# Output turned back by pairs of channels in the two depthwise convolutions of a ConvNeXt-like block

## The chip, the cores and the metric

One core of one Trainium2 chip runs the kernel. The metric is the time of one execution on the device in microseconds.

## What is computed

x has 16 images of 96 channels of 56 x 56 pixels, fp32. Two layers follow each other:

```python
y = depthwise_conv_7x7(x, dw_w) + dw_b               # padding 3
y = layernorm_over_channels(y) * ln_w + ln_b
y = gelu(y @ w1 + b1)                                # 96 -> 384
y = gamma * (y * nx) + beta + y                      # nx: norm over pixels by its mean over channels
y = x + (y @ w2 + b2)                                # 384 -> 96
xq = clip(floor(y * 2**16) / 2**16)
out = depthwise_conv_3x3(xq, power_of_two(w)) + bq   # padding 1
```

## The kernel before

The program has three stages, and each goes through DRAM: the first convolution with running mean and variance over the channels (results in `y_scratch` and `stats_scratch`), the two matrix products by images (`z_scratch`), and the second convolution (`out`). The change touches the convolutions alone. PE is TensorE, DVE is VectorE, ACT is ScalarE, POOL is GpSimd and SP is SyncE, which issues most transfers.

Both convolutions are written by functions of the same names with a stage `S` (`"a"` the first, `"c"` the second). A depthwise convolution goes channel by channel over all images. A **batch** is four channels, there are 24 batches, and `p`, the batch number's lowest bit, picks one of two buffers. For each channel:

- SP loads its rows into `xin` (L369). PE turns the input (`tin`, L636) for two channels at a time: 16 transposes, each of a half of the array, the two halves one beside the other, into PSUM banks 0 and 1. ACT copies and rounds the turned input to `xt_h` (L788, two halves of the images), and DVE takes the low part `xt_l` = turned input minus `xt_h` (L995, two halves).
- `convolve` (L641) does the passes (L664): matrix products of 112 x 128 tables with 464 columns of turned input, over the full array. The first convolution has 12 passes a channel, the second 4. PSUM banks 2 and 3 take the channels in turn.
- ACT copies the result to `yt` with the bias (`yt_copy`, L800). In the second convolution the fourth channel of a batch is copied by DVE (L1195).
- `back` (L676, transposes at L682) turns the output: 8 transposes of half an array. It is called two channels later (`two_before`, L303). Its result lies in PSUM banks 4 and 5, in the second convolution by turns in 4, 5 and 6, 7.
- The turned output is copied to `ost`: in the first convolution by ACT (L807), in the second by DVE (L1187), 112 partitions x 448. From there it is stored (L364), in the second convolution the odd channels by a queue of ACT.
- In the first convolution DVE updates mean and deviation for each channel (L1019, L1021, L1023) and POOL sums the squares (L557); ACT rounds the tables (L815) and POOL takes their low part (L542). In the second POOL casts the tables of a batch (L599).

The order of work is written out by hand for each engine in a `body` over the four channels `s` of a batch, and engines meet at semaphores. `TURN` says that the inputs of the next batch's first two channels are turned at `s` = 0, those of the other two at `s` = 2. On PE the waits for what comes after a channel's passes, `back_waits` and `tin_waits`, stand ahead of its last pass:

```python
for n, (k, w, v) in enumerate(todo):
    if n == len(todo) - 1:
        for q in backs:
            back_waits(*q)
        for q in then_turn:
            tin_waits(*q)
```

`tin_waits` waits for the loaded input and, since the banks of the turned input are the same each time, for DVE's low part (L995) of the inputs turned before (semaphore `xt`).

Of the kernel before, what the change touches and what calls it, by code (L numbers as in the profile page):

```python
# [26 lines left out]
ACT = mybir.ActivationFunctionType  # L27
# [67 lines left out]
def build(nc, x, dw_w, dw_b, ln_w, ln_b, w1, b1, grn_gamma, grn_beta, w2, b2, cw, cb, out):  # L95
# [8 lines left out]
    with ExitStack() as ctx:  # L104
# [195 lines left out]
            low, high = slice(0, LSTEP), slice(LSTEP, TW)  # L300
            return ((to[:, 1:RP], odd[:, 0:RP - 1], slice(0, TW)), (to[low, 0], even[low, 0], low), (to[high, 0], odd[high, RP - 1], high))

        def two_before(b, s, p):  # L303

            return (b, s - 2, p) if s >= 2 else (b - 1, s + 2, 1 - p)

        def rows_group(p, s):

            return ost[:, p, s, :].rearrange("p (n r w) -> p n r w", r=2, w=W)

        def evicted(eng, S, b, s):
# [48 lines left out]

        def store_channel(eng, S, dst, b, k, p):

            eng.wait_ge(S["out"], CB * b + k + 1)
            eng.dma_start(image_runs(dst, CB * b + k), ost[:, p, k, :]).then_inc(S[f"st{p}"], 16)  # L364

        def load_runs(eng, src, c, images, p, k, done):
# [20 lines left out]
        def _(sp):  # L387
# [35 lines left out]
            def conv_transfers(S, src, dst, tables):  # L423

                def store(b, k, p):
                    if S is stages["a"] or k % 2 == 0:
                        store_channel(sp, S, dst, b, k, p)

                def body(it, first, last):
                    for p in range(2):  # L430
                        b = 2 * it + p
                        for k in range(CB):
                            if not last:
                                need(sp, S["tin"], 2 * b + k // 2 + 1)
                                load_channel(S, src, b + 2, k, p)
                                if k == 0:
                                    tables(b + 2, p)
                            if k >= 2 and not (first and p == 0):
                                store(b - 1, k - 2, 1 - p)
                            if k < 2 and not first:  # L440
                                store(b - 2, k + 2, p)
                body(0, True, False)
                with sp.Fori(1, NBODY - 2) as it:
                    body(it, False, False)
                body(NBODY - 2, False, False)
                body(NBODY - 1, False, True)
                for n in range(C - 6, C):
                    b, k = divmod(n, CB)
                    store(b, k, b % 2)

# [153 lines left out]
        def _(pe):  # L604
# [13 lines left out]
            def conv_stage(S, kt, slot0, parts, between=None):  # L618
# [49 lines left out]

                outs = p_back["a" if S is stages["a"] else "c"]

                def back_waits(b, s, p):

                    evicted(pe, S, b, s)
                    need(pe, S["out"], CB * b + s + 1 - len(outs))

                def back(b, s, p):  # L676

                    for h in range(RP):
                        for r in range(2):
                            q = LSTEP * r  # L680
                            row = (h + r) % RP if S is stages["a"] else h + r
                            mm = nc.tensor.transpose(outs[s % len(outs)][0:NM, r, W * h:W * h + W],  # L682
                                                     yt[q:q + W, p, s, row], ident[q:q + W, q:q + W])
                    mm.then_inc(S["back"], 1)

                for u in range(2):
# [3 lines left out]
                def body(it, first, last):  # L690
                    for p in range(2):
                        b = 2 * it + p
                        if between and first and p == 1:
                            between()
                        for s in range(G):
                            turns = TURN0 if first and p == 0 else TURN
                            if not (last and p == 1):
                                for u in turns[s]:
                                    tin(b + 1, u, 1 - p)
                            then_turn = [(b + 1, u, 1 - p) for u in turns[s + 1]] if s + 1 < G else [(b + 2, u, p) for u in TURN[0]]  # L700
                            if last and (p == 1 or s + 1 == G):
                                then_turn = []
                            backs = [] if first and p == 0 and s < 2 else [two_before(b, s, p)]
                            convolve(b, s, p, backs, then_turn)
                            for q in backs:
                                back(*q)
                bodies(pe, body)
                for s in (2, 3):
                    back_waits(NBATCH - 1, s, 1)
                    back(NBATCH - 1, s, 1)  # L710


            conv_stage(stages["a"], KA, 0, ((toep_h, xt_h), (toep_h, xt_l), (toep_l, xt_h)), bias_products)


            pe.wait_ge(stages["a"]["out"], C)
            pe.wait_ge(stat_in, 1)
            for g in range(G):
                for r in range(2):
# [44 lines left out]
        def _(act):  # L764
# [14 lines left out]
            def conv_stage(S, bias, scale, rows_too):  # L779
# [10 lines left out]
                def yt_copy(b, s, p):  # L790
                    n = CB * b + s
                    act.wait_ge(S["conv"], n + 1)
                    if isinstance(b, int) and b == 0 and s == 0 and rows_too:
                        act.wait_ge(bias_in, 16)
                    need(act, S["back"], n + 1 - 2 * CB)
# [7 lines left out]
                def out_copy(b, s, p):  # L803
                    act.wait_ge(S["back"], G * b + s + 1)
                    if s == 0:
                        need(act, S[f"st{p}"], 32 * (b - p))
                    nc.scalar.activation(rows_group(p, s), forwards(p_back["a"][0][0:NM], RP), ACT.Identity).then_inc(S["out"], 1)  # L807

                def table_high(b, s, p):
                    if isinstance(b, int) and b == 0:  # L810
# [14 lines left out]
                def body(it, first, last):  # L825
                    for p in range(2):
                        b = 2 * it + p
                        for s in range(G):
                            if not (last and p == 1):
                                for u in (TURN0 if first and p == 0 else TURN)[s]:  # L830
                                    xt_copy(b + 1, u, 1 - p)
                                if rows_too:
                                    for q in (AHEAD0 if first and p == 0 else AHEAD)[s]:
                                        table_high(b + 1, q, 1 - p)
                            if rows_too or s < CB - 1:
                                yt_copy(b, s, p)
                            if rows_too and not (first and p == 0 and s < 2):
                                out_copy(*two_before(b, s, p))
                            if not rows_too and s % 2 and not (first and p == 0):
                                store_channel(act, S, out_v, b - 1, s, 1 - p)  # L840
                bodies(act, body)
                if rows_too:
                    for s in (2, 3):
                        out_copy(NBATCH - 1, s, 1)
# [65 lines left out]
        def _(dve):  # L910
# [269 lines left out]

            S = stages["c"]

            def out_copy(b, s, p):
                dve.wait_ge(S["back"], G * b + s + 1)
                if s == 0:
                    need(dve, S[f"st{p}"], 32 * (b - p))
                dve.tensor_copy(rows_group(p, s), forwards(p_back["c"][s % 2][0:NM], RP)).then_inc(S["out"], 1)  # L1187

            def yt_copy(b, p):
                s = CB - 1  # L1190
                n = CB * b + s
                dve.wait_ge(S["conv"], n + 1)
                need(dve, S["back"], n + 1 - 2 * CB)
                for to, cols, part in turned_back(S, s, p):
                    ins = dve.tensor_scalar(to, cols, -1.0 / FIX, bias_c[part, bass.ds(n, 1)], ALU.mult, ALU.add)  # L1195
                ins.then_inc(S["ytd"], 1)

            def last_batch(b, s, p):
                if s == CB - 1:
                    yt_copy(b, p)  # L1200
                if not (isinstance(b, int) and b == 0 and s < 2):
                    out_copy(*two_before(b, s, p))
            conv_stage(S, last_batch)
            for s in (2, 3):
                out_copy(NBATCH - 1, s, 1)


_INS = ["x", "L0_conv_dw_w", "L0_conv_dw_b", "L0_conv_ln_w", "L0_conv_ln_b", "L0_conv_w1", "L0_conv_b1",
# [19 lines left out]
```

## Time and profile before

| | |
|---|---|
| median of 3 runs | 1029.27 us (1028.33 to 1031.36) |
| profiled execution, its own time | 1031.37 us |
| span in its profile | 1029.5 us |
| PE busy, share of the span | 966.0 us, 94% |
| DVE | 812.9 us, 79% |
| ACT | 764.0 us, 74% |
| POOL | 415.1 us, 40% |
| chain of work that ended last | PE 87%, DMA 4%, DVE 4%, ACT 2% |
| read and written in DRAM | 129.77 MB, 58.25 MB |

Busy shares are means over three stages with different limits, so each stage is to be read by itself. "PEld" is the loading of weights, which runs beside the matrix products. The granted clock is told as a share of 2.4 GHz (1.00) with 1.2 GHz as 0.50. "Idle before" an instruction names what released it. The chain is followed back from the last instruction, at each step to what released it.

### The profile page before, as it was taken

How to read it: one execution, taken by the hardware profiler on the slowest of the kernel's cores; microseconds unless marked ns; L12 is line 12 of the kernel's file. 1: busy time of each engine (PE TensorE's matmuls, PEld its weight loads, DVE VectorE, ACT ScalarE, POOL GpSimd, SP SyncE). 2: the span in 40 equal slices, each digit the busy share in tenths (PEclk: the TensorE clock that was granted, in tenths of full speed). 3: DMA queues.
4: the chain of work that ended last, by engine and by line, in shares of the span. 5: the costliest groups of instructions: out<-in, count | busy, mean ns of one | idle time of the engine just before them, and what ended most of it. 6: DMA issues, size and time to landing. Idle time of an engine off the chain costs nothing.

```text
span 1029.5 us, 22791 instructions
## 1 busy us (share of the span) xinstructions
PE 966.0 (94%) x6342; PEld 693.0 (67%) x6342; DVE 812.9 (79%) x1477; ACT 764.0 (74%) x1379; POOL 415.1 (40%) x357
## 2 busy tenths in 40 slices
PE   5899999999999378999999999999999985999998
PEld 4688888888888266666666666666666633777775
DVE  5678888888888577888888888888888685777876
ACT  3688888888887366799888888899888832666664
POOL 2567777777777145333323333333323110111110
PEclk9899999999999776999999999999999997999999
DMA  7566666666663392555555555555553244899995
GB/s 188 148 206 204 198 192 194 199 194 199 198 199 124 104 248 70 175 165 170 167 169 173 165 162 160 162 173 170 165 172 109 81 141 147 278 294 293 296 297 177
DMA packets 110260, 188.47 MB, mean 183 GB/s; under 512 B 17357, under 2 KB 104036, under 8 KB 107268
## 3 DMA queue, kind: packets, MB, share of 16 engines
q1 hardware_dynamic: 99988, 173.55, 57.2%
q10 hardware_dynamic: 10240, 14.53, 4.7%
q8 instruction: 15, 0.25, 0.1%
q14 instruction: 17, 0.14, 0.1%
HBM read 129.77 MB, written 58.25 MB: 183 GB/s over the span
## 4 chain that ended last, share of the span: by engine, by line
PE 87%; DMA 4%; DVE 4%; ACT 2%; issue 1%; SPq 1%; POOL 1%; ACTq 0%; DVEq 0%; POOLq 0%
PE psum L664 35%; PE psum L740 23%; PE psum L682 7%; PE psum L730 6%; PE psum L731 6%; PE psum L732 6%; PE psum L636 4%; DMA arena<-lines_a 1%; DMA arena_r<-y_scratch 1%; ACT arena L858 1%; DMA arena_r<-stats_scratch 1%; DMA z_scratch<-arena 1%; DVE arena L1082 0%; POOL arena_r L568 0%; DMA lines_a<-arena 0%
## 5 line engine op out<-in xcount | busy, mean ns | idle before, releaser
L664 PE MATMUL psum<-arena_r 112*128 112x464 f32 x1536 | 382.5, 391 | 10.0 <-DVE arena_r L995 6.0
L664 PEld LDWEIGHTS psum<-arena_r 112*128 112x128 f32 x1536 | 277.6, 191 | 56.6 <-issue 9.5
L740 PE MATMUL psum<-arena,w2s 128*96 128x448 f32 x672 | 268.1, 544 | 2.8 <-DVE w2s L1107 2.8
L891 ACT ACTIVATE arena<-psum,b1g 128x448 f32<-128x448 f32 x336 | 202.1, 630 | 61.0 <-PE psum L732 61.0
L568 POOL TENSOR_TENSOR arena_r<-arena,arena_r 96x448 fp32r<-96x448 f32 x112 | 136.6, 1220 | 266.2 <-DVE arena_r L1068 234.6
L740 PEld LDWEIGHTS psum<-arena,w2s 128*96 128x96 f32 x672 | 110.3, 164 | 120.4 <-issue 113.2
L730 PE MATMUL psum<-arena_r,w1h 96*128 96x448 f32 x336 | 153.5, 457 | 15.6 <-POOL arena_r L568 15.6
L800 ACT ACTIVATE arena<-psum,bias_a 64x112 f32<-64x112 f32 (+1 forms) x288 | 107.6, 407 | 64.0 <-PE psum L664 51.1
L557 POOL TENSOR_TENSOR arena<-arena 128x448 f32<-128x448 f32 x96 | 110.5, 1151 | 98.3 <-DVE arena L1023 98.3
L788 ACT ACTIVATE arena_r<-psum 112x448 fp32r<-112x448 f32 x192 | 93.4, 542 | 65.1 <-PE psum L636 61.6
L858 ACT ACTIVATE arena<-arena 128x1792 bf16<-128x1792 f32 (+1 forms) x91 | 136.8, 1503 | 2.7
L995 DVE TENSOR_TENSOR arena_r<-psum,arena_r 112x448 fp32r<-112x448 f32 x192 | 110.3, 615 | 24.8 <-ACT arena_r L788 24.7
L542 POOL TENSOR_TENSOR arena_r<-arena,arena_r 112x512 fp32r<-112x512 f32 x96 | 122.9, 1291 | 16.1 <-ACT arena_r L815 16.1
L731 PE MATMUL psum<-arena_r,w1h 96*128 96x448 f32 x336 | 125.9, 375 | 0.0
L732 PE MATMUL psum<-arena_r,w1l 96*128 96x448 f32 x336 | 125.5, 373 | 0.0
L1019 DVE TENSOR_TENSOR arena<-arena,psum 128x448 f32<-128x448 f32 x96 | 59.3, 618 | 63.9 <-ACT arena L800 63.7
L682 PEld LDWEIGHTS psum<-ident,arena 56*112 56x112 f32 x1536 | 57.2, 131 | 60.4 <-issue 57.8
L1115 DVE TENSOR_TENSOR psum<-arena,psum 96x448 f32<-96x448 f32 x112 | 69.6, 622 | 33.5 <-PE psum L740 33.1
L730 PEld LDWEIGHTS psum<-arena_r,w1h 96*128 96x128 f32 x336 | 65.4, 195 | 37.3 <-POOL arena_r L568 17.4
L1023 DVE SCALAR_TENSOR_TENSOR arena<-arena,ck 128x448 f32<-128x448 f32 x96 | 89.9, 937 | 0.0
L599 POOL CAST arena_r<-arena 112x1024 fp32r<-112x1024 bf16 x24 | 25.0, 1042 | 156.5 <-PE psum L664 135.6
L682 PE MATMUL psum<-ident,arena 56*112 56x56 f32 x1536 | 81.9, 226 | 3.2 <-ACT arena L807 2.3
(100 smaller groups left out, 1082.2 us busy)
## 6 DMA issues: line engine op xcount, KB each, us to landing
arena<-in_x_dram SPq DMA_DIRECT2D x95, 224.0 KB, 5.1
arena<-lines_a SPq DMA_DIRECT2D x46, 448.0 KB
arena<-z_scratch SPq DMA_DIRECT2D x87, 224.0 KB, 4.6
y_scratch<-arena SPq DMA_DIRECT2D x96, 196.0 KB, 4.8
arena<-in_x_dram SPq DMA_DIRECT2D x112, 168.0 KB, 2.6
z_scratch<-arena SPq DMA_DIRECT2D x112, 168.0 KB, 2.0
arena_r<-y_scratch SPq DMA_DIRECT2D x98, 168.0 KB, 2.6
arena_r<-stats_scratch SPq DMA_DIRECT2D x98, 168.0 KB, 3.1
```

The lines of the kernel that those rows point to most:

```text
L542: pool.tensor_tensor(toep_l[:, p, s, :], toep[:, p, s, :], toep_h[:, p, s, :].bitcast(F32), ALU.subtract).then_inc(A["tl"], 1)
L557: pool.tensor_tensor(m2, m2, dsq[:, k % 2, :], ALU.add).then_inc(m2_done, 1)
L568: pool.tensor_tensor(yl[:, CH * t:CH * t + CH], ct[:, (t + p) % 2, :], yh[:, CH * t:CH * t + CH].bitcast(F32), ALU.subtract).then_inc(yn_r ...
L664: mm = nc.tensor.matmul(p_conv[s % 2][:, 0:NCOL], w[:, p, s, TW * k:TW * k + TW], v[:, p, s, slot0 + k:slot0 + k + JP, :].rearrange("p j i ...
L682: mm = nc.tensor.transpose(outs[s % len(outs)][0:NM, r, W * h:W * h + W], yt[q:q + W, p, s, row], ident[q:q + W, q:q + W])
L730: nc.tensor.matmul(p_h[m][:, 0:CH], w1h[:, w], yh[:, cols], start=True, stop=False)
L731: nc.tensor.matmul(p_h[m][:, 0:CH], w1h[:, w], yl[:, cols], start=False, stop=False)
L732: nc.tensor.matmul(p_h[m][:, 0:CH], w1l[:, w], yh[:, cols], start=False, stop=True).then_inc(h_done, 1)
L740: mm = nc.tensor.matmul(p_o[k][0:C, 0:CH], w2s[:, p, m, :], hid[p][:, m, CH * t:CH * t + CH], start=(m == 0), stop=(m == MT - 1))
L858: nc.scalar.activation(sqd[:, 0:CH * (t1 - t0)], hid[p][:, m, CH * t0:CH * t1], ACT.Square, accum_out=ss[:, p, m, part:part + 1]).then_inc ...
L891: nc.scalar.activation(hid[p][:, m, CH * t:CH * t + CH], p_h[m][:, 0:CH], ACT.Gelu, bias=b1g[:, m:m + 1]).then_inc(gelu_done, 1)
L995: dve.tensor_tensor(turned(xt_l, p, u, half), in_bank(S, b, u, half), turned(xt_h, p, u, half).bitcast(F32), ALU.subtract).then_inc(S["xt" ...
```

## The change

The turn of output goes by pairs. `back` takes a pair `u` of a batch: 16 transposes, channels 2u and 2u + 1, into the two banks side by side (8 x 56 columns of each). It is called after the second and the fourth channel only, for the pair whose second channel is two channels back (`pair_before`). The output copies take a pair at once (112 x 896), by the same engines, and count on the semaphore `out` once a pair. SP's stores of a batch move to the loads two batches later. The numbers of transposes, passes and stores are the same.

```diff
-        def two_before(b, s, p):
-            return (b, s - 2, p) if s >= 2 else (b - 1, s + 2, 1 - p)
-        def rows_group(p, s):
-            return ost[:, p, s, :].rearrange("p (n r w) -> p n r w", r=2, w=W)
+        def pair_before(b, s, p):
+            return (b, 0, p) if s == CB - 1 else (b - 1, 1, 1 - p)
+        def rows_group(p, u):
+            return ost[:, p, 2 * u:2 * u + 2, :].rearrange("p k (n r w) -> p (k n) r w", r=2, w=W)
...
-            eng.wait_ge(S["out"], CB * b + k + 1)
+            eng.wait_ge(S["out"], 2 * b + k // 2 + 1)
...
-                            if k >= 2 and not (first and p == 0):
-                                store(b - 1, k - 2, 1 - p)
-                            if k < 2 and not first:
-                                store(b - 2, k + 2, p)
+                            if not first:
+                                store(b - 2, k, p)
...
-                def back_waits(b, s, p):
-                    evicted(pe, S, b, s)
-                    need(pe, S["out"], CB * b + s + 1 - len(outs))
+                def back_waits(b, u, p):
+                    if S is stages["c"] and u == 1:
+                        evicted(pe, S, b, 2)
+                    evicted(pe, S, b, 2 * u + 1)
+                    need(pe, S["out"], 2 * b + u + 1 - len(outs))
...
+                    for k in range(2):
+                        for h in range(RP):
+                            for r in range(2):
+                                q = LSTEP * r
+                                row = (h + r) % RP if S is stages["a"] else h + r
+                                at = W * (RP * k + h)
+                                mm = nc.tensor.transpose(outs[u % len(outs)][0:NM, r, at:at + W],
+                                                         yt[q:q + W, p, 2 * u + k, row], ident[q:q + W, q:q + W])
                     mm.then_inc(S["back"], 1)
...
-                            backs = [] if first and p == 0 and s < 2 else [two_before(b, s, p)]
+                            backs = [] if s % 2 == 0 or first and p == 0 and s == 1 else [pair_before(b, s, p)]
...
-                            if rows_too and not (first and p == 0 and s < 2):
-                                out_copy(*two_before(b, s, p))
+                            if rows_too and s % 2 and not (first and p == 0 and s == 1):
+                                out_copy(*pair_before(b, s, p))
...
-                dve.tensor_copy(rows_group(p, s), forwards(p_back["c"][s % 2][0:NM], RP)).then_inc(S["out"], 1)
+                dve.tensor_copy(rows_group(p, u), forwards(p_back["c"][u][0:NM], 2 * RP)).then_inc(S["out"], 1)
```

PE in the second convolution, first two channels of batch 22, before (L636 is the turn of input, L664 a pass, L682 the turn of output; `c_xt` is DVE's low part, `c_yt` and `c_ytd` the copies to `yt`):

```order
L636 MATMUL psum<-ident,arena 112x64 x16
L664 MATMUL psum<-arena_r 128x464 [waits c_yt,c_xt,c_th]
L664 MATMUL psum<-arena_r 128x464 x2
L664 MATMUL psum<-arena_r 128x464 [waits c_out,c_yt]
L682 MATMUL psum<-ident,arena 112x56 x8
L664 MATMUL psum<-arena_r 128x464 [waits c_ytd]
L664 MATMUL psum<-arena_r 128x464 x2
L664 MATMUL psum<-arena_r 128x464 [waits c_x11,c_xt,c_out,c_ytd]
L682 MATMUL psum<-ident,arena 112x56 x8
L636 MATMUL psum<-ident,arena 112x64 x16
```

and with the change (L634, L662, L684 are the same lines):

```order
L634 MATMUL psum<-ident,arena 112x64 x16
L662 MATMUL psum<-arena_r 128x464 [waits c_yt,c_xt,c_th]
L662 MATMUL psum<-arena_r 128x464 x3
L662 MATMUL psum<-arena_r 128x464 [waits c_ytd]
L662 MATMUL psum<-arena_r 128x464 x2
L662 MATMUL psum<-arena_r 128x464 [waits c_x11,c_out,c_xt,c_ytd,c_yt]
L684 MATMUL psum<-ident,arena 112x56 x16
L634 MATMUL psum<-ident,arena 112x64 x16
```

The eight transposes between the channels are now part of the sixteen behind the second; the wait for `c_xt` ahead of the last pass stays where it was.

DVE in the second convolution, from the fourth channel of batch 0 to the end of batch 1, before (L995 low part, L1187 output copy, L1195 copy of the fourth channel):

```order
L1195 TENSOR_SCALAR arena<-psum,bias_c 128x560 [waits c_conv]
L1187 COPY arena<-psum 112x448 [waits c_back]
L995 TENSOR_TENSOR arena_r<-psum,arena_r 112x2x28x8 [waits c_xh] x2
L1187 COPY arena<-psum 112x448 [waits c_back] x2
L995 TENSOR_TENSOR arena_r<-psum,arena_r 112x2x28x8 [waits c_xh] x2
L1187 COPY arena<-psum 112x448 [waits c_back]
L1195 TENSOR_SCALAR arena<-psum,bias_c 128x560 [waits c_conv]
L1187 COPY arena<-psum 112x448 [waits c_back]
```

and with the change:

```order
L1195 TENSOR_SCALAR arena<-psum,bias_c 128x560 [waits c_conv]
L1187 COPY arena<-psum 112x896 [waits c_back]
L995 TENSOR_TENSOR arena_r<-psum,arena_r 112x2x28x8 [waits c_xh] x2
L1187 COPY arena<-psum 112x896 [waits c_back]
L995 TENSOR_TENSOR arena_r<-psum,arena_r 112x2x28x8 [waits c_xh] x2
L1195 TENSOR_SCALAR arena<-psum,bias_c 128x560 [waits c_conv]
L1187 COPY arena<-psum 112x896 [waits c_back]
```

The output copies have 896 elements a partition and are half as many; where one copy stood ahead of a pair of low parts and one behind it, all of it now stands ahead.

## Rows read from the trace of the kernel before

**Rows 1.** Busy time by stage: window, length, engines (x instructions), PEclk, DMA share, GB/s.

```profile
60.00:340.00 280.00, 280.00 (x2361) 228.38 (x2357) 227.32 (x338) 224.70 (x504) 200.76 (x169) 1.00 0.63 189
404.00:830.00 426.00, 425.35 (x1564) 274.51 (x1562) 355.72 (x736) 374.98 (x585) 133.75 (x113) 1.00 0.53 156
880.00:1010.00 130.00, 130.00 (x1566) 93.71 (x1568) 103.22 (x177) 81.32 (x139) 20.13 (x20) 1.00 0.93 293
```

**Rows 2.** Chain of waits, first convolution: start us, us, what.

```profile
205.73 2.72 PE psum L664 x12
208.46 0.36 PE psum L682 x8
...
212.34 2.71 PE psum L664 x12
```

**Rows 3.** Timeline, start of the first convolution: start us, us, engine, line, operation.

```profile
18.34 5.45 PE L664 MATMUL psum<-arena_r 112*128 112x464 f32 x24
...
23.71 0.30 PEld L682 LDWEIGHTS psum<-ident,arena 56*112 56x112 f32 x8 [0.32 <-issue]
```

**Rows 4.** Timeline, second convolution, one batch of four channels.

```profile
901.19 1.11 PE L664 MATMUL psum<-arena_r 112*128 112x464 f32 x4
...
902.23 0.42 PE L682 MATMUL psum<-ident,arena 56*112 56x56 f32 x8
902.44 0.52 PEld L636 LDWEIGHTS psum<-ident,arena 64*112 64x112 f32 x16
...
902.67 0.57 ACTq L364 DMA_DIRECT2D out_dram<-arena  x1
902.70 0.62 DVE L1187 COPY arena<-psum 112x448 f32<-112x448 f32 x1 [0.44 <-PE psum L682]
...
903.03 1.10 PE L664 MATMUL psum<-arena_r 112*128 112x464 f32 x4
...
903.35 0.98 ACT L788 ACTIVATE arena_r<-psum 112x448 fp32r<-112x448 f32 x2
903.92 1.15 DVE L995 TENSOR_TENSOR arena_r<-psum,arena_r 112x448 fp32r<-112x448 f32 x2 [0.60 <-ACT arena_r L788]
...
905.13 0.19 PEld L664 LDWEIGHTS psum<-arena_r 112*128 112x128 f32 x1 [0.20 <-DVE arena_r L995]
905.54 0.30 PEld L682 LDWEIGHTS psum<-ident,arena 56*112 56x112 f32 x8 [0.23 <-issue]
...
905.76 0.53 PEld L636 LDWEIGHTS psum<-ident,arena 64*112 64x112 f32 x16
...
905.85 0.80 DVE L1195 TENSOR_SCALAR arena<-psum,bias_c 128x560 f32<-128x560 f32 x1 [0.24 <-PE psum L664]
...
906.55 0.98 ACT L788 ACTIVATE arena_r<-psum 112x448 fp32r<-112x448 f32 x2 [1.48 <-PE psum L636]
906.57 0.61 DVE L1187 COPY arena<-psum 112x448 f32<-112x448 f32 x1
...
908.81 0.42 PE L682 MATMUL psum<-ident,arena 56*112 56x56 f32 x8
```

**Rows 5.** Timeline, first convolution, POOL and DVE.

```profile
207.30 1.30 POOL L542 TENSOR_TENSOR arena_r<-arena,arena_r 112x512 fp32r<-112x512 f32 x1
...
207.83 1.25 DVE L1023 SCALAR_TENSOR_TENSOR arena<-arena,ck 128x448 f32<-128x448 f32 x1
...
214.42 0.68 DVE L1023 SCALAR_TENSOR_TENSOR arena<-arena,ck 128x448 f32<-128x448 f32 x1
```

**Rows 6.** Groups of instructions by shape: busy us, mean ns of one, idle before.

```profile
L1187 DVE COPY arena<-psum 112x448 f32<-112x448 f32 x96 | 59.1, 616 | 13.5 <-PE psum L682 13.5
...
L807 ACT ACTIVATE arena<-psum 112x448 f32<-112x448 f32 x96 | 52.4, 546 | 3.5 <-PE psum L682 1.2
...
L1082 DVE SCALAR_TENSOR_TENSOR arena<-arena 128x1344 f32<-128x1344 f32 x2 | 3.1, 1546 | 0.0
```

**Rows 7.** Who waited for whom, 880 to 1000 us: us, times, longest.

```profile
PEld psum L664 <- DVE arena_r L995: 4.3, 18, 0.3
```

More of the change, by code:

```diff
@@ L446, in conv_transfers @@
                 body(NBODY - 1, False, True)
-                for n in range(C - 6, C):
+                for n in range(C - 2 * CB, C):
                     b, k = divmod(n, CB)
@@ L669, in conv_stage, with back @@
                 outs = p_back["a" if S is stages["a"] else "c"]
-                def back_waits(b, s, p):
-                    evicted(pe, S, b, s)
-                    need(pe, S["out"], CB * b + s + 1 - len(outs))
[L676 to L683, printed above, removed]
+                def back_waits(b, u, p):
[3 more added lines that the diff above has]
+                    need(pe, S["out"], 2 * b + u + 1 - len(outs))
+                def back(b, u, p):
+                    for k in range(2):
[6 more added lines that the diff above has]
+                                                         yt[q:q + W, p, 2 * u + k, row], ident[q:q + W, q:q + W])
                     mm.then_inc(S["back"], 1)
@@ L707, in conv_stage @@
                 bodies(pe, body)
-                for s in (2, 3):
-                    back_waits(NBATCH - 1, s, 1)
-                    back(NBATCH - 1, s, 1)
+                back_waits(NBATCH - 1, 1, 1)
+                back(NBATCH - 1, 1, 1)
             conv_stage(stages["a"], KA, 0, ((toep_h, xt_h), (toep_h, xt_l), (toep_l, xt_h)), bias_products)
-            pe.wait_ge(stages["a"]["out"], C)
+            pe.wait_ge(stages["a"]["out"], 2 * NBATCH)
             pe.wait_ge(stat_in, 1)
@@ L794, in yt_copy @@
                         act.wait_ge(bias_in, 16)
-                    need(act, S["back"], n + 1 - 2 * CB)
+                    need(act, S["back"], 2 * b + s // 2 - 3)
                     if S is stages["a"]:
@@ L801, in yt_copy, with out_copy @@
                     ins.then_inc(S["yt"], 1)
-                def out_copy(b, s, p):
-                    act.wait_ge(S["back"], G * b + s + 1)
-                    if s == 0:
+                def out_copy(b, u, p):
+                    act.wait_ge(S["back"], 2 * b + u + 1)
+                    if u == 0:
                         need(act, S[f"st{p}"], 32 * (b - p))
-                    nc.scalar.activation(rows_group(p, s), forwards(p_back["a"][0][0:NM], RP), ACT.Identity).then_inc(S["out"], 1)
+                    nc.scalar.activation(rows_group(p, u), forwards(p_back["a"][0][0:NM], 2 * RP), ACT.Identity).then_inc(S["out"], 1)
                 def table_high(b, s, p):
@@ L842, in conv_stage @@
                 if rows_too:
-                    for s in (2, 3):
-                        out_copy(NBATCH - 1, s, 1)
+                    out_copy(NBATCH - 1, 1, 1)
                 else:
@@ L1181, in _, with out_copy @@
             S = stages["c"]
-            def out_copy(b, s, p):
-                dve.wait_ge(S["back"], G * b + s + 1)
-                if s == 0:
+            def out_copy(b, u, p):
+                dve.wait_ge(S["back"], 2 * b + u + 1)
+                if u == 0:
                     need(dve, S[f"st{p}"], 32 * (b - p))
-                dve.tensor_copy(rows_group(p, s), forwards(p_back["c"][s % 2][0:NM], RP)).then_inc(S["out"], 1)
+                dve.tensor_copy(rows_group(p, u), forwards(p_back["c"][u][0:NM], 2 * RP)).then_inc(S["out"], 1)
             def yt_copy(b, p):
@@ L1192, in yt_copy @@
                 dve.wait_ge(S["conv"], n + 1)
-                need(dve, S["back"], n + 1 - 2 * CB)
+                need(dve, S["back"], 2 * b + s // 2 - 3)
                 for to, cols, part in turned_back(S, s, p):
@@ L1200, in last_batch @@
                     yt_copy(b, p)
-                if not (isinstance(b, int) and b == 0 and s < 2):
-                    out_copy(*two_before(b, s, p))
+                if s % 2 and not (isinstance(b, int) and b == 0 and s == 1):
+                    out_copy(*pair_before(b, s, p))
             conv_stage(S, last_batch)
-            for s in (2, 3):
-                out_copy(NBATCH - 1, s, 1)
+            out_copy(NBATCH - 1, 1, 1)
 _INS = ["x", "L0_conv_dw_w", "L0_conv_dw_b", "L0_conv_ln_w", "L0_conv_ln_b", "L0_conv_w1", "L0_conv_b1",
```

## The prediction

> **What bounds the kernel now.** I read the stages first [rows 1]: the first convolution (60 to 340 us), the two matrix products (404 to 830) and the second convolution (880 to 1010). PE is busy all the time in each, at a granted clock of 1.00, the upper of its two levels. DVE and ACT lie at about 0.81 in the first convolution; in the second DVE is at 0.79 (103.22 of 130.00) and the DMA engines at 0.93. The chain of waits says the same: in the first convolution it is PE from end to end [rows 2]. So a microsecond off PE's program counts there in full, until another engine's part of the loop becomes longer than PE's.
>
> PE's time has a cost at each change of kind. Twelve passes take 2.72 us until the turn of output begins, a lone turn of output (eight transposes) 0.36, and two channels with their turns 6.61 [rows 2]. In the second convolution four passes take 1.04 (901.19 to 902.23), and a turn of output that an input's turn follows takes 0.21 (902.23 to 902.44), not 0.36, so 0.14 to 0.15 is the way back to passes [rows 4]. Eight passes more (12 against 4) cost 2.72 - 1.04 = 1.68, or 0.21 each; hence 0.20 of a group's time is its own beginning and end: 2.72 - 12 x 0.21, and the same for 1.04. Only once do 24 passes stand in a row: 5.37 us (18.34 to 23.71) with one idle stretch of 0.32 at their end [rows 3], where 24 x 0.21 + 0.20 is 5.24.
>
> **The change, first convolution.** For each pair of channels one turn of output between passes goes, and its eight transposes join the others. Removed: 0.36 for the lone turn and 0.20 for the second group's beginning and end; added: 0.21 for eight transposes in the long run. That is -0.35 from these rows; rounding of the 0.20 leaves -0.34, which I take. If the one long run [rows 3] is right, with 5.37 for 24 passes, it is only -0.21. So a pair goes from 6.61 to 6.27, bounds 6.27 to 6.40.
> The output copy on ACT becomes one of 896 elements a row instead of two of 448 at 0.546 [rows 6]; it costs at most twice that, so ACT's work does not grow. It stands behind the second channel's copy and ahead of the next input copy. ACT's busy work is 0.80 x 13.2 = 10.6 us of a batch, which now takes 12.5, and 24 passes give the input copies and DVE's low part 5 us before they are wanted. Stores are issued up to two channels later, but the output buffer too is refilled a channel later. I cost all these at nothing; their cover is the length of the passes. DVE and POOL have a queue of their own: DVE's third update step takes 1.25 us when POOL's table subtraction runs beside it (207.30, 207.83) and 0.68 when not (214.42) [rows 5]. At 10.7 us of DVE work (227.32 / 280.00 x 13.2) in a batch of 12.5 that still fits. There are 48 pairs; 47 have a lone turn, and about two of them lie in the first batches, where PE waits for others. **-0.34 x 45 = -15.3 us**, bounds -9.5 (0.21) and -16.
>
> **Second convolution.** PE's own work falls alike: eight passes take 1.04 + 4 x 0.21 = 1.88, sixteen transposes of output 0.43, the input's turn until the next pass 0.59 (902.44 to 903.03): 2.90 a pair. But here something else stands close behind. The last pass of a pair waits until DVE's low part of the input turned before is done, because the next input goes into the same PSUM bank. Already now that wait ends last in every batch [rows 7]: weight load at 905.13, right after the two low parts end at 905.07 [rows 4]. Behind each such load the next turn begins 0.41 later (905.13 to 905.54).
> Now the new order, counted from Z, the begin of the turns of output (902.23 and 905.54 in the rows) [rows 4].
> Pair whose last copy is ACT's: DVE's output copy began at Z + 0.47 (902.70) and begins now, behind eight more transposes, at Z + 0.68. It reads 896 elements. No copy of that length is in the trace: 448 take 0.616, and another DVE instruction of 1344 takes 1.546 [rows 6]. 896 more elements cost 0.93 there, so 448 more are 0.465 and the copy is 1.08; bounds 1.01 (if half of 0.93 is somewhat high) and 1.23 (twice 0.616). DVE starts the next instruction some 0.05 before the end of one, so it is free at Z + 1.71. ACT's input copy needs the turned input: 0.79 from the input turn's begin (905.76 to 906.55) to a copy not held by anything, so Z + 0.43 + 0.79 = Z + 1.22 (before, at 903.35, it was held by the issue of a store, begun at 902.67, until Z + 1.12). DVE's low parts follow 0.57 behind it (903.35 to 903.92): Z + 1.79, end at + 1.15 = Z + 2.94, weight load at + 0.06 = Z + 3.00, next turn at + 0.41 = **Z + 3.41**.
> Pair whose last channel is copied by DVE itself: that copy starts at Z + 0.31 (905.54 to 905.85) and holds DVE for 0.72 (until 906.57), then the output copy for 1.03: Z + 2.06. The low parts end at Z + 3.21, the load comes at 3.27, the next turn at **Z + 3.68**.
> So a batch takes 7.09 instead of 6.58 (902.23 to 908.81): +0.51, although PE alone would need 5.80. The gain is not only hidden but turned round: one long copy stands where a short one stood, ahead of the low part that PE waits for, and PE has one turn less to fill the time. Batches 1 to 22: 22 x 0.51 = +11.2. Batches 0 and 23 have about three pairs without this wait: -0.34 x 3 = -1.0. The end gets a copy longer by 0.47 and two stores that start together instead of one after the other, +1.0 together by estimate. **+11.2 us**, bounds +9 (copy 1.01) and +16 (copy 1.23).
> The Trainium skill ("VectorE: DVE Perf Modes", the TRN2 errata) puts a copy from PSUM at 120 cycles plus one per element at 0.96 GHz. By it the long copy would be 1.06, and the sum about 1 us lower; for 448 elements it gives 0.59, where the row has 0.616, so I stay with the row.
>
> **Matrix products:** untouched, 0. The handover between first convolution and products ends with the same number of elements copied, 0.
>
> **Sum:** -15.3 + 11.2 = -4.1 us. The profiled execution took 1031.37 (span 1029.5), so it would be 1027.3; its time lies 2.1 above the median of the three runs, 1029.27, and the forecast for a median is 1029.27 - 4.1 = **1025.2 us**. Its own range is 1021 to 1029.
>
> **The rivals.**
> *Copy at twice the price.* The long copy crosses two pairs of rows in PSUM banks and costs 1.23: in the first kind of pair DVE is then free at Z + 1.86 instead of ACT's 1.79, +0.07, in the other +0.15, x 22 = +4.8: 1030.0. For it: DVE's 560-element instruction takes 0.80 (905.85), more than the 0.73 that my slope gives (0.616 + 112 x 0.00104). Against: its operation and pattern are others.
> *PE alone decides.* Both convolutions gain. The second would then run against the transfers: 293 GB/s at a share of 0.93 [rows 1] are 1.93 MB a batch; at a share of 1.0 and 315 GB/s a batch is 6.13, -0.45 x 23 = -10.4, and the sum is -15.3 - 10.4 = -25.7: 1003.6. This is what follows from the rule in the Trainium skill ("TensorEngine Tiling (Array Packing)", Key Properties) that each change of tiling mode drains TensorE, if nothing else held PE. The 0.32 idle at each such change [rows 3] agrees with it. Against the gain in the second convolution: DVE already ends last there [rows 7].
> *DVE and POOL take over in the first convolution* (the other side). If the passes are shorter, POOL's table subtractions fall on more of DVE's third steps; two more of a batch at 1.25 instead of 0.68 raise DVE's 10.7 to 11.9 of 12.5 us, and with the waits between its steps PE comes to wait for its low parts here too. The decision point is 12.73 us a batch: above it the first convolution saves less than the second loses. At 13.0 it is -0.2 x 24 + 11.2 = +6.4: 1035.7. For it: DVE's step is stretched in two of four channels now. Against: DVE and POOL have idle time of 19% and 28%.
> *No saving by joining:* the idle 0.32 belongs to passes, not to changes; the first convolution stays, the second loses its 11.2: 1040.5. The run of 24 passes with one such gap speaks against it.
>
> **How the numbers follow.** About 0.3% (3.1 us) is what a measurement tells from no change. Forecast 0.60 (0.50 of it faster by more than that, 0.10 within it); copy at twice the price 0.17 (0.13 within, 0.04 slower); PE alone 0.08 (faster); DVE and POOL 0.12 (slower); no saving 0.03 (slower). Faster 0.58, same 0.23, slower 0.19. For the range I leave out PE alone, no saving and the outer ends, and keep DVE and POOL: 1018 to 1035.
>
> **What would show it.** First convolution: 12.5 us a batch, a run of 24 passes of about 5.25 us, no PE wait for low parts. Second: 7.0 to 7.2 us a batch, the long copy at 1.08, the last weight load of each pair waiting 0.5 to 0.8 us for DVE's low part, DMA share down to about 0.86. I am wrong if a batch of the second convolution is below 6.5, or one of the first above 12.7.

## The result, and the profile after

| | before | after |
|---|---|---|
| median | 1029.73 us (7 runs) | 1024.65 us (7 runs, 1023.92 to 1025.81) |
| ratio | | 0.9948, 95% interval 0.9936 to 0.9961 |
| span in the profile | 1029.5 us | 1023.5 us |

The kernel became 5 us (0.5%) faster; 4.1 were forecast. It is a small difference of two large terms, as forecast: in the profiled executions the first convolution gained 13.8 us, the second lost 8.0, and the span fell by 6.0. The chain that ended last in the changed kernel, as shares of the span:

```profile
PE 77%; DVE 9%; issue 4%; DMA 4%; ACT 3%; SPq 1%; DVEq 1%; POOL 1%; ACTq 0%; POOLq 0%
```

The chain held PE for 87% of the span before and holds it for 77% now; DVE rose from 4% to 9% and "issue" from 1% to 4%. Something other than PE has begun to end waits. The two convolutions tell where (as in [rows 1]):

```profile
60.00:325.00 265.00, 265.00 (x2328) 227.00 (x2327) 224.58 (x336) 216.64 (x459) 201.14 (x167) 1.00 0.66 200
...
870.00:1000.00 130.00, 118.56 (x1484) 89.32 (x1485) 94.40 (x131) 77.02 (x131) 19.88 (x19) 1.00 0.91 280
```

In the first convolution PE still has no gap. In the second PE is busy for 118.56 of 130.00 us, where it had all 130.00, and the transfers went from 293 to 280 GB/s: the stage runs slower with less traffic, so what holds it is inside the core.

**First convolution.** The chain of waits of the changed kernel, one pair of channels and the start of the next, against [rows 2]:

```profile
198.72 5.25 PE psum L662 x24
203.97 0.58 PE psum L684 x16
204.55 0.48 PE psum L634 x16
205.03 5.26 PE psum L662 x24
```

The 24 passes take 5.25, sixteen transposes of output 0.58 and the input's turn 0.48: 6.31 from start to start, where it was 6.61. The stage's end shows the sum. ACT's table load for the square root, which stands behind the last output copy, in the changed kernel:

```profile
332.86 1.28 ACT L868 ACT_TABLE_LOAD   x1
```

and in the kernel before:

```profile
346.67 1.28 ACT L868 ACT_TABLE_LOAD   x1
```

It comes 13.8 us earlier. In the eight other runs below that have the same first convolution it comes between 330.7 and 334.6, so this figure is good to about 2 us; the 0.30 a pair (three pairs in a row take 6.31, 6.29 and 6.29) is the firmer one.

**Second convolution.** The timeline of one batch of the changed kernel, the same place as [rows 4]:

```profile
893.20 0.65 PE L684 MATMUL psum<-ident,arena 56*112 56x56 f32 x16
...
893.52 0.80 DVE L1195 TENSOR_SCALAR arena<-psum,bias_c 128x560 f32<-128x560 f32 x1 [0.78 <-PE psum L662]
...
894.24 1.08 DVE L1187 COPY arena<-psum 112x896 f32<-112x896 f32 x1
...
894.46 0.98 ACT L789 ACTIVATE arena_r<-psum 112x448 fp32r<-112x448 f32 x2 [1.52 <-PE psum L634]
895.24 1.15 DVE L995 TENSOR_TENSOR arena_r<-psum,arena_r 112x448 fp32r<-112x448 f32 x2
...
896.44 0.19 PEld L662 LDWEIGHTS psum<-arena_r 112*128 112x128 f32 x1 [0.82 <-DVE arena_r L995]
...
896.84 0.65 PE L684 MATMUL psum<-ident,arena 56*112 56x56 f32 x16
...
897.53 1.09 DVE L1187 COPY arena<-psum 112x896 f32<-112x896 f32 x1 [1.15 <-PE psum L684]
...
898.00 0.98 ACT L789 ACTIVATE arena_r<-psum 112x448 fp32r<-112x448 f32 x2 [0.23 <-PE psum L634]
898.58 1.16 DVE L995 TENSOR_TENSOR arena_r<-psum,arena_r 112x448 fp32r<-112x448 f32 x2
...
899.79 0.19 PEld L662 LDWEIGHTS psum<-arena_r 112*128 112x128 f32 x1 [0.57 <-DVE arena_r L995]
...
900.20 0.65 PE L684 MATMUL psum<-ident,arena 56*112 56x56 f32 x16
```

From Z = 893.20 to the next turn of output at 896.84 are 3.64 us, and 3.36 more to 900.20. In the first pair DVE copies the fourth channel (893.52), then the output (894.24, 1.08 long), and only then takes the low parts (895.24 to 896.39); the last weight load follows at 896.44. In the second pair the output copy ends at 898.62, just when ACT's first half is ready, and the low part starts at 898.58. The view of who waited for whom, 870 to 995 us, sums it (us, times, longest). PE's weight loads now wait for the low part in every pair; in [rows 7] it was 4.3 us, 18 times, once a batch:

```profile
PEld psum L662 <- DVE arena_r L995: 25.2, 36, 0.9
...
PE psum L662 <- DVE arena_r L995: 11.3, 36, 0.5
```

The batch is best read over twenty of them, from DVE's copies of the fourth channel. After:

```profile
865.52 0.80 DVE L1195 TENSOR_SCALAR arena<-psum,bias_c 128x560 f32<-128x560 f32 x1 [0.64 <-PE psum L662]
...
1005.33 0.80 DVE L1195 TENSOR_SCALAR arena<-psum,bias_c 128x560 f32<-128x560 f32 x1 [0.78 <-PE psum L662]
```

Before:

```profile
879.15 0.80 DVE L1195 TENSOR_SCALAR arena<-psum,bias_c 128x560 f32<-128x560 f32 x1 [0.18 <-PE psum L664]
...
1011.67 0.80 DVE L1195 TENSOR_SCALAR arena<-psum,bias_c 128x560 f32<-128x560 f32 x1 [0.23 <-PE psum L664]
```

That is 139.81 / 20 = 6.99 us after and 132.52 / 20 = 6.63 before. The long copies of DVE and ACT in the changed kernel (mean ns of one behind the busy time):

```profile
L1187 DVE COPY arena<-psum 112x896 f32<-112x896 f32 x48 | 52.0, 1086 | 26.7 <-PE psum L684 26.7
...
L808 ACT ACTIVATE arena<-psum 112x896 f32<-112x896 f32 x48 | 44.2, 921 | 2.0 <-PE psum L684 0.8
```

### The profile page after: what moved, and what is told of

It reads as the page before. It is cut to its first block, busy times and chain, and to the rows that moved or that the text cites. A ratio compares the mean times of both kernels' runs of the same rounds, so it can differ in the third digit from the quotient of the medians.

```text
span 1023.5 us, 22653 instructions
## 1 busy us (share of the span) xinstructions
PE 947.0 (93%) x6342; PEld 694.0 (68%) x6342; DVE 806.2 (79%) x1429; ACT 757.1 (74%) x1331; POOL 416.3 (41%) x357
## 4 chain that ended last, share of the span: by engine, by line
PE 77%; DVE 9%; issue 4%; DMA 4%; ACT 3%; SPq 1%; DVEq 1%; POOL 1%; ACTq 0%; POOLq 0%
PE psum L662 27%; PE psum L741 23%; PE psum L731 6%; PE psum L732 6%; PE psum L733 6%; PE psum L684 5%; DVE arena_r L995 4%; PE psum L634 3%; DVE arena L1187 2%; ACT arena_r L789 1%; DMA arena_r<-y_scratch 1%; DMA arena<-lines_a 1%; ACT arena L858 1%; DMA arena_r<-stats_scratch 1%; DMA z_scratch<-arena 1%
## 5 line engine op out<-in xcount | busy, mean ns | idle before, releaser
L662 PE MATMUL psum<-arena_r 112*128 112x464 f32 x1536 | 368.3, 387 | 23.3 <-DVE arena_r L995 19.8
L662 PEld LDWEIGHTS psum<-arena_r 112*128 112x128 f32 x1536 | 285.1, 191 | 79.3 <-DVE arena_r L995 27.8
L995 DVE TENSOR_TENSOR arena_r<-psum,arena_r 112x448 fp32r<-112x448 f32 x192 | 110.1, 615 | 12.3 <-ACT arena_r L789 12.3
L597 POOL CAST arena_r<-arena 112x1024 fp32r<-112x1024 bf16 x24 | 25.1, 1046 | 164.6 <-PE psum L662 144.1
L1023 DVE SCALAR_TENSOR_TENSOR arena<-arena,ck 128x448 f32<-128x448 f32 x96 | 89.0, 927 | 0.0
L865 ACT ACTIVATE arena<-arena,cvec 96x448 f32<-96x448 f32 x112 | 73.8, 661 | 11.0 <-DMA arena<-in_x_dram 7.2
L634 PE MATMUL psum<-ident,arena 64*112 64x64 f32 x1536 | 63.2, 225 | 17.3 <-DMA arena<-z_scratch 9.1
```

The lines of the kernel that those rows point to most:

```text
L662: mm = nc.tensor.matmul(p_conv[s % 2][:, 0:NCOL], w[:, p, s, TW * k:TW * k + TW], v[:, p, s, slot0 + k:slot0 + k + JP, :].rearrange("p j i ...
L995: dve.tensor_tensor(turned(xt_l, p, u, half), in_bank(S, b, u, half), turned(xt_h, p, u, half).bitcast(F32), ALU.subtract).then_inc(S["xt" ...
```

## The experiments

All are timed beside the kernel before on the same chip, and the ratio is to that kernel there; its median there was 1030.43 to 1031.57 us, and 1029.73 beside the changed kernel, so ratios compare better than times.

**Each convolution by itself.** The functions take their group size from the stage (here only the rule for the turns is shown; the second kernel has `False` and `True` in the first line):

```diff
+        WIDE = {"a": True, "c": False}
...
+        def turned_out(S, b, s, p, first):
+            if wide(S):
+                return [] if s % 2 == 0 or first and p == 0 and s == 1 else [(b, 0, p) if s == CB - 1 else (b - 1, 1, 1 - p)]
+            return [] if first and p == 0 and s < 2 else [(b, s - 2, p) if s >= 2 else (b - 1, s + 2, 1 - p)]
```

> Turns of output by pairs in the first convolution alone; the second as before. My theory: the first convolution gains 0.6 us a batch (12.6 instead of 13.2), and the second loses 7 to 8 us in the changed kernel through the long copy ahead of DVE's low part. So this kernel takes about 1029.7 - 13.8 = 1016 us, with batches of the second convolution at 6.6 us. Rival: the gain is spread over both convolutions and is about 5 us in all, with nothing lost anywhere: then this one takes 1025 to 1027.

> Turns of output by pairs in the second convolution alone. My theory: 13.2 us a batch in the first convolution, 7.0 in the second, about 1029.7 + 8 = 1038 us. Rival, that joining turns pays or is neutral in the second convolution too: 1025 to 1030.

The first convolution alone took 1016.22 us, ratio 0.9857 (0.9833 to 0.9880). The second alone took 1036.87, ratio 1.0064 (1.0039 to 1.0088). The twenty batches of the second convolution, with single turns:

```profile
865.23 0.80 DVE L1227 TENSOR_SCALAR arena<-psum,bias_c 128x560 f32<-128x560 f32 x1 [0.17 <-PE psum L686]
...
996.95 0.80 DVE L1227 TENSOR_SCALAR arena<-psum,bias_c 128x560 f32<-128x560 f32 x1 [0.16 <-PE psum L686]
```

and with pairs:

```profile
877.84 0.80 DVE L1227 TENSOR_SCALAR arena<-psum,bias_c 128x560 f32<-128x560 f32 x1 [0.63 <-PE psum L686]
...
1016.72 0.80 DVE L1227 TENSOR_SCALAR arena<-psum,bias_c 128x560 f32<-128x560 f32 x1 [0.68 <-PE psum L686]
```

They are 6.59 and 6.94 us a batch. So the change is a gain in one stage and a loss in the other, and half of it is the faster kernel: a ratio of 0.9857 against 0.9948. That falsifies the rival of a small gain spread over both. By the medians of before on this chip (1031.57) the first kernel gained 15.4 us and the second lost 5.3, where 13.8 and 8 had been expected. The two ratios together make 0.9920, the changed kernel has 0.9948; the intervals are too wide to tell these apart. The batches show the loss more firmly: 0.35 us each, over 22 of them close to 8 us.

**What gains in the first convolution.** PE turns each channel's output by itself again; ACT still copies pairs.

```diff
-                    for k in range(2):
+                    for k in ks:
...
+                            if S is stages["a"]:
+                                backs = [] if first and p == 0 and s < 2 else [(b, 0, p, (s - 2,)) if s >= 2 else (b - 1, 1, 1 - p, (s,))]
                             convolve(b, s, p, backs, then_turn)
```

> The changed kernel, but in the first convolution PE turns the output of each channel by itself again, eight transposes behind each channel's passes, while ACT still copies pairs (896 elements). My theory: the gain of the first convolution is PE's change between passes and transposes alone, so a batch is back at 13.2 us and the kernel at 1024.7 + 13.8 = 1038 us. Rival: the gain comes from fewer and longer copies on ACT: 1025 us.

It took 1038.46 us, ratio 1.0071 (1.0052 to 1.0090); the changed kernel's is 0.9948, 1.2% lower. Its chain of waits:

```profile
205.04 2.72 PE psum L662 x12
207.76 0.36 PE psum L688 x8
208.12 2.72 PE psum L662 x12
210.84 0.36 PE psum L688 x8
211.20 0.45 PE psum L634 x16
211.65 2.71 PE psum L662 x12
```

6.61 us a pair again, although ACT's 48 copies of 896 elements take 0.92 us here too.

The fewer and longer copies bring PE nothing; the number of changes between passes and transposes is what pays. The idle time of the weight loads ahead of the turns of output, which the view of waits puts down to "issue", counts these changes. From 60 to 320 us it is, in the kernel before:

```profile
PEld psum L682 <- issue: 24.8, 78, 0.3
```

with the change:

```profile
PEld psum L684 <- issue: 13.1, 41, 0.3
```

and 25.1 us in 79 of them in this kernel. That is 0.32 us for each change that is gone, near the 0.30 that a pair saves. The rule of the Trainium skill ("TensorEngine Tiling (Array Packing)", Key Properties) that changing the tiling mode drains TensorE agrees with it. The waits at semaphores ahead of a turn went with each change too; no run separates their part.

**What loses in the second.** DVE takes the low part ahead of the long output copy:

```diff
             def last_batch(b, s, p):
                 if s == CB - 1:
                     yt_copy(b, p)
-                if s % 2 and not (isinstance(b, int) and b == 0 and s == 1):
-                    out_copy(*pair_before(b, s, p))
+                if s % 2 == 0 and not (isinstance(b, int) and b == 0):
+                    out_copy(b - 1, s // 2, 1 - p)
```

> The changed kernel with DVE's low part ahead of the long output copy in the second convolution. My theory: PE waits for the low part, and the long copy ahead of it is what costs; without it the low part waits for ACT's copy of the input alone, so every pair takes the 3.36 to 3.41 us that now only one kind of pair takes: 6.7 to 6.8 us a batch instead of 7.0, 1019 to 1021 us. Still slower in the second convolution than before the change (6.6). Rival: the wait follows the turn of input whatever stands ahead: 7.0, 1024.7 us.

This missed. It took 1033.45 us, ratio 1.0023 (1.0012 to 1.0035), with 7.39 us a batch. Its timeline from one turn of output on:

```profile
899.46 1.08 DVE L1187 COPY arena<-psum 112x896 f32<-112x896 f32 x1
...
900.00 0.65 PE L684 MATMUL psum<-ident,arena 56*112 56x56 f32 x16
...
900.72 0.58 ACTq L364 DMA_DIRECT2D out_dram<-arena  x1
...
901.50 0.98 ACT L789 ACTIVATE arena_r<-psum 112x448 fp32r<-112x448 f32 x2 [2.04 <-PE psum L634]
...
902.08 1.16 DVE L995 TENSOR_TENSOR arena_r<-psum,arena_r 112x448 fp32r<-112x448 f32 x2 [0.83 <-ACT arena_r L789]
...
903.28 0.19 PEld L662 LDWEIGHTS psum<-arena_r 112*128 112x128 f32 x1 [0.90 <-DVE arena_r L995]
```

The output copy now ends late, at 900.54. On ACT the store of an odd channel waits for it (ACTq, 900.72 to 901.30), and ACT's input copy stands behind that store: it starts at Z + 1.50 (900.00 to 901.50), not at Z + 1.16 as in the changed kernel (896.84 to 898.00). The low part that was to come earlier came later. I had moved an instruction on one engine without asking who waits for it on another. So the next kernel also takes the stores out of the way:

```diff
-                            if not rows_too and s % 2 and not (first and p == 0):
-                                store_channel(act, S, out_v, b - 1, s, 1 - p)
+                            if not rows_too and s == 2 and not (first and p == 0):
+                                store_channel(act, S, out_v, b - 1, 1, 1 - p)
+                            if not rows_too and s == 0 and not first:
+                                store_channel(act, S, out_v, b - 2, 3, p)
```

> As the kernel with the low part ahead of the long copy (1033 us, slower), but ACT's stores of the odd channels are issued two channels later, when the copy they need is long done. In that kernel's trace the store's issue on ACT waits for the long copy and the input copy (Z + 1.50 instead of Z + 1.16) starts behind it. Theory: with the store out of the way the low part starts at Z + 1.8, every pair takes 3.36 to 3.41 us, a batch 6.8, the kernel 1019 to 1021 us. Rival: something else of that order holds the input copy: 7.2 us or more a batch, 1030 us.

1020.50 us, ratio 0.9901 (0.9882 to 0.9920), 6.78 us a batch. The timeline:

```profile
901.55 0.64 PE L684 MATMUL psum<-ident,arena 56*112 56x56 f32 x16
...
902.81 0.98 ACT L789 ACTIVATE arena_r<-psum 112x448 fp32r<-112x448 f32 x2 [1.51 <-PE psum L634]
...
903.38 1.16 DVE L998 TENSOR_TENSOR arena_r<-psum,arena_r 112x448 fp32r<-112x448 f32 x2 [0.59 <-ACT arena_r L789]
...
904.59 0.19 PEld L662 LDWEIGHTS psum<-arena_r 112*128 112x128 f32 x1 [0.63 <-DVE arena_r L998]
...
905.00 0.65 PE L684 MATMUL psum<-ident,arena 56*112 56x56 f32 x16
```

The input copy starts at Z + 1.26 (901.55 to 902.81), the low parts 0.57 behind it, the last load comes at 904.59, and the next turn at Z + 3.45. The long copy ahead of the low part thus costs about 0.2 us a batch, and the batch is still 0.15 longer than with single turns. What remains, 6.78 against the 5.8 that the prediction reckoned for PE alone, is the chain turned input, ACT's copy, DVE's low part, last pass. DVE already stands idle for 0.59 us ahead of the low part, so no earlier place on DVE would shorten it.

**Taking that chain away.** The second convolution gets two pairs of PSUM banks for the turned input, by `u`, and one pair for the turned output:

```diff
-            return psum[:, 4 * u:4 * u + 2, :] if isinstance(b, int) and b == 0 else p_in
+            if S is stages["c"]:
+                return psum[:, 6 * u:6 * u + 2, :]
+            return psum[:, 4 * u:4 * u + 2, :] if isinstance(b, int) and b == 0 else p_in
...
-        p_back = {"a": [psum[:, 4:6, :]], "c": [psum[:, 4:6, :], psum[:, 6:8, :]]}
+        p_back = {"a": [psum[:, 4:6, :]], "c": [psum[:, 4:6, :]]}
...
-                    need(pe, S["xt"], 4 * b + 2 * u - (2 if isinstance(b, int) and b == 0 else 0))
+                    need(pe, S["xt"], 4 * b + 2 * u - (2 if S is stages["c"] or isinstance(b, int) and b == 0 else 0))
```

> The changed kernel with two pairs of PSUM banks for the turned input in the second convolution and one, instead of two, for the turned output. PE need not wait any more for the low part of the input turned just before. My theory: the joined turns then save PE time there too; PE alone would need 5.8 to 5.9 us a batch, the transfers at a share of 1.0 about 6.1, so 6.0 to 6.2 us a batch and 1004 to 1006 us. If transfers do not bind: 1000 us. If the low part's wait is not the cause of the loss: 7.0 us and 1024.7, or more through the single pair of output banks.

> The kernel with two pairs of input banks once more, on the same chip as the one with stores first: 1004 to 1010 us, batches of the second convolution uneven at 6.1 to 6.3 us on average.

1007.19 us, ratio 0.9773 (0.9735 to 0.9812), and on the second chip 1005.96, ratio 0.9753 (0.9724 to 0.9782): faster than both kernels, though the first run lies a little above the 1004 to 1006 us expected. Its batches take 6.26 and 6.22 us on average, and they are uneven (5.81 to 8.37 us in the first run). Some waits now end with transfers (865 to 975 us):

```profile
DVE arena L1189 <- DMA out_dram<-arena: 3.0, 5, 1.1
PE psum L664 <- DMA arena<-z_scratch: 2.9, 3, 1.4
```

The next kernel leaves out the stores of each batch's first channel, so a quarter of the output is not written. It serves only to measure:

```diff
-                    if S is stages["a"] or k % 2 == 0:
+                    if S is stages["a"] or k == 2:
...
-                    need(dve, S[f"st{p}"], 32 * (b - p))
+                    need(dve, S[f"st{p}"], 24 * (b - p))
```

> The kernel with two pairs of input banks (1007 us), with the stores of each batch's first channel of the second convolution left out (a quarter of its output is not written; 0.2 of 1.94 MB a batch). Theory: transfers bind there, its batches are uneven (5.8 to 8.4 us, 6.26 on average) and with fewer bytes come to PE's own 5.8 to 5.9: 998 to 1000 us. Rival: the single pair of output banks binds it: unchanged, 1007.

998.61 us, ratio 0.9683 (0.9665 to 0.9701). Its copies of the fourth channel, twenty batches apart:

```profile
863.57 0.80 DVE L1197 TENSOR_SCALAR arena<-psum,bias_c 128x560 f32<-128x560 f32 x1
...
980.55 0.80 DVE L1197 TENSOR_SCALAR arena<-psum,bias_c 128x560 f32<-128x560 f32 x1 [0.36 <-PE psum L664]
```

That is 5.85 us a batch, and none of the twenty is above 6.04. The stretch 865 to 975 us (PE, PEld, DVE, ACT, POOL busy, clock, DMA share, GB/s), with all stores:

```profile
865.00:975.00 110.00, 105.80 (x1411) 84.18 (x1411) 88.67 (x123) 73.15 (x124) 17.82 (x18) 1.00 0.94 304
```

and with three quarters of them:

```profile
865.00:975.00 110.00, 110.00 (x1507) 90.25 (x1507) 94.90 (x133) 78.36 (x133) 19.15 (x19) 1.00 0.95 300
```

PE is busy without a gap in the second. So transfers take the rest of the gain, 0.4 us a batch. Whether it is their amount or the time until a single store has freed its buffer this kernel does not separate: fewer stores change both. With the low part and a quarter of the stores out of the way a pair takes 0.39 us less than before the change (5.85 against 6.63 a batch). The joined turns, 0.30 in the first convolution, and the wait of [rows 7] would account for it; how it divides was not measured.

Two kernels around it. One puts the stores on SP ahead of the loads:

> The kernel with two pairs of input banks (1007 us), with SP issuing each store of the second convolution ahead of the load beside it instead of behind. Theory: the transfers as a whole bind, so the order changes little: 1004 to 1009 us. If a good part of the uneven batches comes from output copies that wait for stores issued too late, it comes to 1000 to 1003 us.

1007.71 us, ratio 0.9777 (0.9750 to 0.9805), no different within the intervals from 0.9753 on the same chip: it is not this order that binds. Its view of waits (865 to 975 us) helps with the open question. DVE's waits for stores are gone from it, which were 3.0 and 3.5 us in the two runs without this order, and PE's waits for the loads from `z_scratch` are 4.7 us, where they were 2.9 in one of those runs and not listed in the other. Stores that go out earlier delay the loads and the time stays, which speaks for the amount of the transfers, though it does not prove it. The other has the banks with single turns of output, and pairs in the first convolution alone:

> Pairs in the first convolution alone, single turns of output in the second, and there two pairs of PSUM banks for the turned input and one for the output. Theory: with single turns PE's own program takes 6.5 us a batch and the low part's wait is 0.1 at most, so the banks alone bring nothing to speak of: 6.5 to 6.6 us a batch, 1014 to 1016 us, as without them (1016.2). The kernel with pairs and these banks took 1007. If instead the banks themselves are what helps, this one also comes to 1007.

This missed: 1043.45 us, ratio 1.0124 (1.0104 to 1.0143), 7.81 us a batch. It does not tell what it was made for, because it brings a wait of its own, which the expectation had left out: with one pair of output banks and a turn for each channel, PE waits for DVE's copy of the channel before, besides the low part (880 to 1000 us):

```profile
PEld psum L688 <- DVE arena_r L1028: 12.9, 15, 1.0
...
PE psum L688 <- DVE arena L1221: 9.0, 23, 0.6
```

It shows only that two pairs of banks for the input and one for the output are no gain with single turns. The kernel with pairs, where the output copy has a whole pair's time, did gain with the same banks.

## Why the prediction was right

- **Bound.** PE from end to end in the first convolution held, before and after. ACT, DVE and POOL cost nothing there: ACT's long copy took 0.92, below twice 0.546, and DVE's third update step (L1023) 0.93 on average, as before (0.94). The rival in which DVE and POOL take over has no mark in the trace; a batch is 12.6, below the decision point of 12.73.
- **-0.34 a pair, -15.3 in all.** Measured 0.30 (6.61 to 6.31) and 13.8. The 24 passes came at 5.25 as reckoned, and the longer 5.37 of the one run in the old trace was not met. What was undersized is what stands between the runs: eight transposes more and the way back were to make 1.02, and the chain shows 0.58 + 0.48 = 1.06.
- **+0.51 a batch, +11.2.** The place, the order of events and both pairs were right: Z + 3.64 and Z + 3.36, forecast 3.68 and 3.41. But +0.36 was measured, not +0.51, so this term was too large by 3.2 us over the stage. Of the 0.15, 0.10 lies in the batch after, 6.99 instead of 7.09. In the second pair the turned input reached ACT's copy at Z + 1.16, not Z + 1.22, and in the first each of several steps was a little shorter than its row. The other 0.05 lies in the batch before, which was read from a single short one (6.58): the batches alternate, about 6.57 and 6.66, and with one of 6.91 the mean of the twenty is 6.63. That makes +7.3 over the twenty batches shown, and +7.1 from the first copy of a fourth channel (872.64 before, 858.63 after) to the last (1023.59 and 1016.64). From the last to the end of the span it is 5.9 and 6.9 us, +1.0 as estimated.
- **The long copy.** 1.086 us, forecast 1.08. The estimate from the Trainium skill ("VectorE: DVE Perf Modes", the TRN2 errata), 1.06, was slightly low. The rival of twice the price falls.
- **PE alone decides** fell as stated, through DVE's low part; the kernel with two pairs of input banks is that rival with its obstacle removed, and it lands at 1006 to 1007, near the 1003.6 worked out for it, with transfers as the bound that was named.
- **The signs.** Those of PE and DVE came as stated: 12.6 and 6.99 us a batch, weight loads that wait 0.57 and 0.82 us for the low part. The DMA share fell only to 0.91, where 0.86 was forecast, while what they moved fell by 4%, from 293 to 280 GB/s. The share did not follow the rate.
- **The sum.** -13.8 + 7.1 + 1.0 = -5.7; the remaining 0.3 of the span's -6.0 lies between the stages and in rounding. The forecast had -4.1. The first term was oversized by 1.5 and the second by 3.2, with opposite signs, so that the total is off by 1.9 in the profiled executions and by 1.0 in the medians. The mechanism was right in both stages, but that the total came so near is partly luck. The matrix products, which no kernel here changes, show how far an untouched stretch varies: from the table load of the square root to the first copy of a fourth channel, which is nearly all matrix products, it is 522.9 to 526.6 us over the twelve traces, and 525.4 and 524.0 in the two runs of one kernel.

## What to carry to other kernels

Joining short turns of a second kind between long runs of PE work paid here for each change saved, 0.3 us, but only in the stage where nothing stood right behind PE. Before making a unit larger on all engines, count from PE's next wait back: the engine that now copies two units in one go may have work queued behind it that PE needs, and another engine's store may be queued behind the copy. Where a buffer's reuse makes PE wait, a second buffer taken from a place that larger units free (here an output pair of banks) can be worth more than a better order: 6.26 us a batch against 6.78.

## What I had not expected

An order on DVE that brings the low part forward made the kernel slower, a ratio of 1.0023 instead of 0.9948, by way of a DMA issue on ACT: the store's issue waited for the copy now made later, took 0.58 us, and held up an input copy by 0.34. And in the second convolution waits ended with transfers at a share of 0.94 and 304 GB/s, while at 0.95 and 300 GB/s PE had no gap: here the share alone does not tell whether transfers bind; the waits that they end do.
